# Two-part fp32r queries and keys, two heads at a time, for the first layer's cross attention

## The reference

```
x = x + mha(layernorm(x), ctx, ctx)      # first layer, 16 heads of 16 columns, 2048 keys
x = x + state_space(layernorm(x))        # a scan over the 128 rows
x = x + lora_mixture(layernorm(x))
x = x + single_head_attention(layernorm(x), ctx, mask)
x = x + windowed_attention(layernorm(x)) # 16 heads of 128
x = x + mixture_of_experts(layernorm(x)) # 8 experts
```

```
scores = qh @ kh.T / 4                   # 128 queries x 2048 keys, 16 columns deep
scores = where(ki <= qi + 1920, scores, -10000)
out    = softmax(scores) @ vh
```

## Time and profile before

| | us |
|---|---|
| median of 3 runs | 516.42 (515.78 to 519.46) |
| profiled execution, its own time | 518.79 |
| its span, first to last instruction | 516.8 |
| until pass one of group 0 starts | 30.8 |
| pass one of group 0 | 30.8 to 42.5 |
| groups 0 to 7 (pass two) | 42.5 to about 203 |
| PE busy, share of the span | 427.5, 83% |
| DVE busy | 344.4, 67% |
| ACT busy | 269.2, 52% |
| POOL busy | 121.6, 24% |

### The profile page before, as it was taken

How to read it: one execution, slowest core, us unless ns; L and a number is a source line. 1 busy time by engine, 2 the same in 40 slices (tenths; PEclk the granted TensorE clock), 3 DMA queues, 4 the chain that set the end, 5 groups by cost and what they waited for, 6 DMA issues and landing times.

```text
span 516.8 us, 8974 instructions
## 1 busy us (share of the span) xinstructions
PE 427.5 (83%) x3584; PEld 312.8 (61%) x3584; DVE 344.4 (67%) x544; ACT 269.2 (52%) x577; POOL 121.6 (24%) x78
## 2 busy tenths in 40 slices
PE   0177899998787796595989998999599889999997
PEld 0124466665554574434843373445588789999996
DVE  4952766777477964599754756585553599778772
ACT  4314678774678433360313242456784066777762
POOL 4010157000057000090001326241300112333300
PEclk9999889998798699667999999999799979999999
DMA  6599454433510053100740000004900097540000
GB/s 215 132 287 313 153 144 109 114 94 83 129 31 1 1 193 146 51 0 0 305 186 1 1 0 3 0 0 142 346 3 2 18 351 255 192 164 1 2 2 20
DMA packets 27306, 54.11 MB, mean 105 GB/s; under 512 B 5018, under 2 KB 17530, under 8 KB 23931
## 3 DMA queue, kind: packets, MB, share of 16 engines
q1 hardware_dynamic: 27264, 53.54, 32.7%
HBM read 40.65 MB, written 0.26 MB: 79 GB/s over the span
## 4 chain that ended last, share of the span: by engine, by line
PE 57%; DVE 26%; ACT 7%; issue 6%; DMA 2%; POOL 1%; SPq 0%; ACTq 0%; DVEq 0%; POOLq 0%
PE ps L1246 17%; PE ps L1067 8%; DVE mx L1632 5%; PE ps L882 5%; PE ps L869 4%; PE ps L838 3%; DVE reg_b L1423 3%; DVE reg_a L1423 2%; PE ps L1211 2%; ACT reg_b L653 2%; PE ps L1200 2%; PE ps L1201 2%; PE ps L977 1%; PE ps L996 1%; DVE reg_b L1414 1%
## 5 line engine op out<-in xcount | busy, mean ns | idle before, releaser
L1632 DVE TENSOR_REDUCE mx<-ps 128x1 f32<-128x1024 f32 x64 | 76.6, 1221 | 47.7 <-PE ps L838 37.1
L653 ACT ACTIVATE reg_b<-ps 128x512 f32<-128x512 f32 x128 | 75.3, 598 | 41.8 <-PE ps L869 21.9
L869 PE MATMUL ps<-qreg,reg_b 98*128 98x128 bf16 x512 | 51.2, 237 | 5.8 <-ACT reg_b L653 4.5
L869 PEld LDWEIGHTS ps<-qreg,reg_b 98*128 98x128 bf16 x512 | 38.2, 106 | 17.7 <-ACT reg_b L653 7.8
L1246 PE MATMUL ps<-part_a 128*128 128x256 f32 x384 | 48.2, 283 | 0.4 <-DVE part_a L1777 0.4
L1067 PE MATMUL ps<-reg_b,xT 128*128 128x512 f32 x96 | 47.6, 618 | 0.0
L1246 PEld LDWEIGHTS ps<-part_a 128*128 128x128 f32 x384 | 46.9, 192 | 0.6 <-DVE part_a L1777 0.6
L882 PE MATMUL ps<-reg_b 128*32 128x128 f32 x1024 | 46.3, 302 | 0.0
L838 PE MATMUL ps<-reg_b,qreg 96*128 96x512 bf16 x96 | 35.9, 443 | 9.0 <-DVE mx L1632 6.6
L788 ACT ACTIVATE reg_a<-ps,b 128x256 f32<-128x256 f32 x64 | 30.2, 471 | 23.9 <-PE ps L1246 23.9
L377 POOL TENSOR_TENSOR rstd<-ve,cf 128x1 f32<-128x1 f32 x12 | 6.7, 561 | 147.4 <-DVE ve L1319 147.3
(11 more groups left out here) (278 smaller groups left out, 891.6 us busy)
## 6 DMA issues: line engine op xcount, KB each, us to landing
reg_b<-in_w SPq DMA_DIRECT2D x16, 512.0 KB, 7.2
reg_b<-in_w SPq DMA_DIRECT2D x8, 1024.0 KB, 7.1
reg_b<-reg_b SPq DMA_DIRECT2D x56, 128.0 KB, 2.8
reg_b<-in_w_qkv SPq DMA_DIRECT2D x3, 2048.0 KB, 13.2
reg_b<-reg_a SPq DMA_DIRECT2D x40, 128.0 KB, 2.5
reg_a<-in_ctxK SPq DMA_DIRECT2D x4, 1024.0 KB, 7.2
reg_a<-in_ctx SPq DMA_DIRECT2D x2, 2048.0 KB, 10.0
reg_a<-in_ctxT SPq DMA_DIRECT2D x2, 2048.0 KB, 9.7
```

The source lines that it names most:

```text
L653: sc.activation(pT[n % 3], score_b[n % 2], ACT.Exp).then_inc(S("exp_done"), 1)
L869: mm = pe.matmul(cols, kS[g % 3][0:SROWS, c // 8, j, P * (c % 8):P * (c % 8 + 1)], qT[b][0:SROWS, HPG * hg + j, :], start=not last, stop=True)
L1632: ve.reduce_max(mx[:, piece // 2, piece % 2:piece % 2 + 1], score_a[m % 2].rearrange("p i k -> p (i k)"), X_AXIS).then_inc(S("max_done"), 1)
```

## The change

- Q and K are split in two float32r parts, high and low, instead of three bf16 parts. (float32r is a float32 that PE takes in a faster and less exact way.) One head takes 64 rows (`SLOT`): 16 rows whose first two hold ones in K and the negative maximum in Q (the other 14 are zero in Q), then K high by Q high, K high by Q low, K low by Q high. Two heads fill 128 rows.
- `scores_for_max(g, piece)` has 8 pieces, each two heads by 512 keys: one product on rows 0 to 63 and one on rows 64 to 127, into different banks. In the last quarter the mask is 256 columns wide and the products are two of 256 columns for each head. The pieces are issued in four portions of two: `MAX_AT` is `[(-1, 2), (1, 2), (3, 2), (5, 2)]`.
- `scores_shifted` has 2 products of 256 columns for a chunk in place of 4 of 128.
- K's parts: one ACT copy and one DVE subtraction for each half. For batch 1 one ACT copy and one POOL subtraction, four pieces each. SP issues 6 DMAs of 256 KB a group, with group 0's cut in two sets of 6 of 128 KB, so that pass one can start on the first two heads. The three small loads of ones go; in their place DVE sets one `kS` buffer to 1 and POOL the other two, and POOL sets two more tiles of 2048 words to 0.
- Only batch 0's queries are split and transposed (8 transposes of 128x128 float32) ahead of the first group. Batch 1's are split behind group 0's maximum and transposed and copied in groups 2, 3 and 4.

```
-MAX_AT = [(-1, 2), (0, 2), (1, 3), (2, 2), (3, 2), (4, 3), (5, 2)]
-FIRST_AT = [(3, 4), (4, 4), (5, 4), (6, 4)]
+MAX_AT = [(-1, 2), (1, 2), (3, 2), (5, 2)]
+FIRST_AT = [(3, 2), (4, 2), (5, 2), (6, 2)]
...
+            def spread_keys(g, pairs, pieces, name):
+                b, hg = divmod(g, NHG)
+                sp.wait_ge(S("k_high_done"), pieces)
+                for t in range(1, TERMS):
+                    if t == TERMS - 1:
+                        sp.wait_ge(S("k_low_done"), pieces)
+                    src = k_high_raw if t < TERMS - 1 else k_low_raw
+                    for j in range(2):
+                        row = SLOT * j + HD0 * t
+                        sp.dma_start(kS_raw[g % 3][row:row + HD0, pairs, :],
+                                     src[2 * hg + j::2 * NHG, b, pairs, :]).then_inc(S(name), 16)
...
             for g in range(NG):
-                b, hg = divmod(g, NHG)
                 if g >= 3:
                     sp.wait_ge(S("pv_done"), NCH * (g - 2))
-                for part, at in enumerate(((0, 3, 5), (1, 4), (2,))):
-                    sp.wait_ge(S(f"k{part + 1}_done"), (2, 2 + HPG)[b])
-                    for t in at:
-                        for half in range(2):
-                            row = 2 * hg + half
-                            sp.dma_start(kS[g % 3][t:QROWS:PARTS, half, :, :],
-                                         ks3[b][part][row::2 * NHG, :, :]).then_inc(S(f"kS_in{g % 3}"), 16)
+                if g == 0:
+                    sp.wait_ge(S("first_pads"), 1)
+                    spread_keys(0, slice(0, 1), 1, "first_in")
+                    spread_keys(0, slice(1, 2), 2, "kS_in0")
+                else:
+                    if g < 3:
+                        sp.wait_ge(S("pads_set"), 2 + g)
+                    spread_keys(g, slice(0, PAIRS), PAIRS if g < NHG else PAIRS + HPG, f"kS_in{g % 3}")
...
-            for i in range(2):
-                pool.memset(va[i][:, :, :, :], 0.0).then_inc(S("cleared"), 1)
+            pool.memset(part_o[:, :].bitcast(F32), 0.0).then_inc(S("pads_set"), 1)
+            pool.memset(part_q[:, :].bitcast(F32), 0.0).then_inc(S("pads_set"), 1)
+            pool.memset(kS_raw[1], 1.0).then_inc(S("pads_set"), 1)
...
             inv_sqrt(0, 0)
             inv_sqrt(0, 1)
+            pool.memset(kS_raw[2], 1.0).then_inc(S("pads_set"), 1)
+            for i in range(2):
+                pool.memset(va[i][:, :, :, :], 0.0).then_inc(S("cleared"), 1)
...
+            def key_high(u):
+                sc.wait_ge(S(f"ctxK_in{u}"), 16)
+                sc.copy(k_high[:, 0, u, :], ctxK[:, 0, u, :]).then_inc(S("k_high_done"), 1)
...
+            def query_rows(n):
+                sc.wait_ge(S("pads_set"), 2)
+                sc.wait_ge(S("qT_ps"), n + 1)
+                first, count, src = query_slots(n)
+                for j in range(2):
+                    rows = slice(SLOT * j, SLOT * (j + 1))
+                    sc.copy(qT[rows, first:first + count, P * j:P * (j + 1)],
+                            src[rows, :].rearrange("p (s q) -> p s q", s=count)).then_inc(S("qT_sb"), 1)
...
+            def scores_for_max(g, piece):
+                hg = g % NHG
+                u, quarter = divmod(piece, 4)
+                m = 8 * g + piece
...
+                if m >= 2:
                     pe.wait_ge(S("max_done"), m - 1)
+                dst = score_a[m % 2]
+                if quarter == 3:
+                    for j in range(2):
+                        pe.matmul(dst[:, j, 256:512], identb, hide_q, start=True, stop=False)
+                for at in (slice(256, 512), slice(0, 256)) if quarter == 3 else (slice(0, 512),):
+                    keys = slice(512 * quarter + at.start, 512 * quarter + at.stop)
+                    for j in range(2):
+                        rows = slice(SLOT * j, SLOT * (j + 1))
+                        mm = pe.matmul(dst[:, j, at], qT[rows, PAIRS * hg + u, P * j:P * (j + 1)], kS[g % 3][rows, u, keys],
+                                       start=quarter < 3 or at.start == 0, stop=True)
+                mm.then_inc(S("score_a"), 1)
...
-                for j in range(HPG):
-                    cols = score_b[n % 2][:, P * j:P * (j + 1)]
+                for u in range(PAIRS):
+                    cols = score_b[n % 2][:, 2 * P * u:2 * P * (u + 1)]
                     if last:
-                        pe.matmul(cols, identb, hide_k, start=True, stop=False)
-                    mm = pe.matmul(cols, kS[g % 3][0:SROWS, c // 8, j, P * (c % 8):P * (c % 8 + 1)], qT[b][0:SROWS, HPG * hg + j, :],
-                                   start=not last, stop=True)
+                        pe.matmul(cols.rearrange("p (j q) -> p j q", j=2), identb, hide_k, start=True, stop=False)
+                    mm = pe.matmul(cols, kS[g % 3][:, u, P * c:P * (c + 1)],
+                                   qT[:, PAIRS * (g % NHG) + u, :], start=not last, stop=True)
...
-            beside = {(0, 9): [(late_part1, 0)], (0, 11): [(late_part1, 1)], (0, 13): [(late_part1, 2)], (0, 15): [(late_part1, 3)],
-                      (1, 7): [(late_part2, 0)], (1, 9): [(late_part2, 1)], (1, 11): [(late_part2, 2)], (1, 13): [(late_part2, 3)],
+            beside = {(0, 13): [(late_high, 0)], (0, 15): [(late_high, 1)], (1, 1): [(late_high, 2)], (1, 3): [(late_high, 3)],
+                      (2, 8): [(query_rows, 2)], (2, 13): [(query_rows, 3)], (3, 8): [(query_rows, 4)], (4, 7): [(query_rows, 5)],
...
+            ve.memset(kS_raw[0], 1.0).then_inc(S("first_pads"), 1)
             ve.wait_ge(S("x_in"), 32)
             layer_norm(0)
...
+                ve.wait_ge(S("pads_set"), 1)
                 q = tmp[b][:, :].rearrange("p (h d) -> p h d", h=H0)
                 link(ve.tensor_scalar(tmp[b][:, :], xn[b][:, :], 1.0 / math.sqrt(HD0), None, ALU.mult))
+                link(ve.tensor_copy(q_split[b][:, :, 1:4:2, :], q.unsqueeze(2).to_broadcast([P, H0, 2, HD0])))
+                ve.tensor_tensor(q_split[b][:, :, 2, :], q, q_split[b][:, :, 1, :], ALU.subtract)\
                     .then_inc(S("q_split"), 1)
...
-            key_residue(0)
+            key_low(0)
             split_queries(0)
-            key_residue(1)
-            key_part3(0)
-            key_part3(1)
-            split_queries(1)
+            key_low(1)
...
-                    ve.reduce_max(mx[:, piece // 2, piece % 2:piece % 2 + 1],
-                                  score_a[m % 2].rearrange("p i k -> p (i k)"), X_AXIS).then_inc(S("max_done"), 1)
+                    u, quarter = divmod(piece, 4)
+                    ve.reduce_max(mx[:, 2 * u:2 * u + 2, quarter:quarter + 1], score_a[m % 2], X_AXIS)\
+                        .then_inc(S("max_done"), 1)
```

More of the change, by code:

```diff
@@ L29 @@
 NG = NB * NHG
[L30 to L34 removed]
+PAIRS = 2
+SLOT = P // PAIRS
+TERMS = SLOT // HD0
+KEY_DMAS = 2 * (TERMS - 1)
 VW = 32
@@ L404, in state_input @@
                 pool.wait_ge(S("bc_sb"), (8, 20)[b])
+                if b == 0:
+                    for i in range(3):
+                        pool.wait_ge(S(f"kS_in{i}"), 16 * KEY_DMAS * (3, 3, 2)[i])
                 pool.tensor_tensor(state[b][:, h], tmp[b][:, h * P:(h + 1) * P].unsqueeze(1).to_broadcast([P, NS, P]),
@@ new lines, in query_columns @@
+            def query_columns(n):
+                pe.wait_ge(S("q_split"), (1, 1, 2, 2, 2, 2)[n])
+                if n >= 2:
+                    pe.wait_ge(S("o_all"), (2, 2, 3, 4)[n - 2])
+                    pe.wait_ge(S("qT_sb"), 2 * n)
+                first, count, dst = query_slots(n)
+                q = q_raw[n // 2 if n < 2 else 1].rearrange("p (s j) t d -> p s (j t d)", j=2)
+                for i in range(count):
+                    mm = pe.transpose(dst[:, P * i:P * (i + 1)], q[:, first + i, :], ident)
+                mm.then_inc(S("qT_ps"), 1)
@@ L1022, in side_work @@
                     step[0](*step[1:])
-            for part in range(16):
-                scores_for_max(0, part)
+            for piece in range(8):
+                scores_for_max(0, piece)
             max_to_rows(0)
```

194 lines of the change are left out of this document (71 added, 123 removed).

## The result

The changed kernel takes **533.98 us** (median of 4 runs, 532.31 to 536.48) against 517.94 (515.78 to 521.34) for the kernel before: a ratio of 1.031 (95% interval 1.023 to 1.039). It is slower. The forecast was 499, with 0.03 for slower. Its profiled execution took 535.1 us, the span 533.3. Medians are over all runs of a kernel; a ratio compares only its undisturbed ones with those of the kernel before, so the two can differ by some tenths of a per cent.

The account below looks back on a forecast made before the run. It took the uncovered first 42.5 us and then mostly PE in the groups as bounds. Start -12.8 and groups -5.0 make -17.8: 518.8 profiled gives 501.0, forecast 499 us from the 516.4 median; range 487 to 510.

Parts of the forecast that it names:

- What covers the rest of the start: Loads behind the start: values and later keys at 310 GB/s arrive in time, with a cover of 1 to 6 us.
- part 1: Start of the kernel: first product at 17.1 us, transposes of the maxima at 29.8 instead of 42.55, -12.8 us.
- the sum: All groups together -5 us, with group 0 -0.5 and group 1 -1.5; with the start's -12.8, -17.8 in all.
- the DMA queue paces the start: Rival at the start: load covers missed by 9 us in all, giving 508 us; chance 0.05.
- slower rival: Pass one: 64-row float32r products go at plain float32's rate, giving about 596 us; chance 0.03.
- The clock rival: Group borders: PE's waits bring the half clock at four more borders, +12 us, giving 511; chance 0.13.
- The memsets ... on POOL end by about 17 and cost nothing: Start: POOL's memsets of the last `kS` buffer and of `va` end by about 17 us, at no cost.
- Part 2: Pass one on PE: row halves overlap 1.65-fold, -1.2 us a group, against +0.8 for changes into and out of halves.
- halves one after the other: Rival in pass one: the row halves do not overlap, +1.4 us a group, giving 506; chance 0.12.
- Part 3: Pass two's scores: 2 x 256 columns a chunk instead of 4 x 128 cost 0, bounds -0.5 and +0.8 a group.
- Part 4: Four portions in pass one: two reductions follow the last instead of one, +0.7 us a border, for six borders.

Follow-up runs that it names:

- run 5: Changed kernel with each head's terms interleaved over 48 rows and POOL's memsets moved behind the keys' subtractions (also written e5): 511.49 us, ratio 0.987.
- run 1: Changed kernel with only each head's three terms interleaved over 48 rows instead of 16 adjacent rows each (also written e1): 515.94 us, ratio 1.000.
- bf16 stand-in: Run 5 with pass two's score products reading a bf16 unit matrix on both sides, so its scores are not computed: 504.44 us, ratio 0.973.
- reverse edit: Run 5 with pass one's pieces issued in seven visits instead of four portions of two: 504.70 us, ratio 0.974.
- the edit in the old kernel: Kernel before with only its table changed, 16 parts of pass one in four visits of four instead of seven: 521.56 us, ratio 1.006.
- Version 6: Changed kernel with terms spread over 48 rows, POOL's memsets later and seven visits instead of four: 504.70 us, ratio 0.974.

## Why the prediction was wrong

**The step that failed is "What covers the rest of the start"**, with the landing in part 1. It took the landing of a K copy, 2.8 us, from `reg_b<-reg_b SPq DMA_DIRECT2D x56, 128.0 KB`, a row of copies to every sixth row, and carried the 310 GB/s of the earlier trace rows over to copies to 16 adjacent rows. What the runs showed in its place: 174 and 181 GB/s, batch 1's values landed after 35.9 us, and group 2's keys there at 68.2, forecast for 42.6 (61.2 with the memsets late, so most of the delay isn't theirs). I read the size and the number of the transfers in the diff (6 of 256 KB for 12 of 128) and not their rows. The keys came late for groups 1 and 2, PE waited 3.4 and 5.3 us, and the clock did the rest: groups 0 and 1 took 16.0 us more than before, where the sum had -2.0. Undone by itself this gives back 18 us by the medians, 16 by the ratios. Even with the spread rows and the start as forecast (run 5) group 2's keys land at 48.3, 6 us after the forecast: 310 GB/s was too high for them too, but nothing waited. The rival "the DMA queue paces the start" named the right mechanism, at 0.05 and for 9 us, as a gain missed; it could turn the sign, and that case was absent. My slower rival was about float32r in pass one. The clock rival didn't happen at the borders: with the rows spread (run 1), a wait of 1.4 us at the border of groups 0 and 1 left the clock at 1.00, and in the kernel after it is low behind the waits for keys.

**"The memsets ... on POOL end by about 17 and cost nothing"**: they do end at 16.2, and DVE is held until 16.37: 5.6 us at the maximum of group 0 with the slow rows (35.3 to 29.7) and 6.5 without (35.6 to 29.1). I had allowed for a factor of 1.7 on DVE's steps from the two scans; two operations of 0.41 us that last 7.58 are no slowdown by a factor but a wait for the other's end. The Trainium skill ("SBUF — State Buffer", Who interferes with whom) calls the shared port pair an exclusive lock, held for a whole instruction, that a `tensor_scalar` can take. The trace agrees that DVE is shut out rather than slowed, and shows it shut out through three memsets in a row. With the memsets moved, first product and maximum came at 16.1 and 29.2, against 17.1 and 29.8 forecast: the rest of part 1 came out within 1 us, partly by luck: I read 11.43 us for 12 issues as 0.95 each, but an issue takes 0.6, and 4 us of the 11.43 are SP's wait for a part of the keys in the middle of the twelve. The measured start, -7.2, lies outside the bounds that I had given it (-8.5 to -15).

**Part 2** was right in its first half: 0.165 us a product of 512 columns where full-width ones take 0.23, so 1.4-fold for two halves (1.65 forecast); "halves one after the other" is refuted. The price of leaving the halves fits as well: 0.32 us from the last pair's start to the next visit, where 512 columns alone take 0.23, so about 0.1.

**Part 3**, priced at 0, costs 0.13 us a pair (0.67 against 0.54), 1.0 a group at the full clock, just outside its bound of +0.8. The bf16 stand-in returned 7.0 us by the medians, part of it perhaps by way of the clock, and 0.6 to 0.7 in each group at the full clock.

**Part 4** was priced at +0.7 a border, about 4 in all. The reverse edit gave 4.4 in the groups (0.5 to 0.8 in each one at the full clock) and 6.8 in the medians, the edit in the old kernel cost 3.1: right in size. Its place was partly another: ACT's idle 1.15 us behind a masked portion.

**The sum, mended.** The medians make a ladder: 533.98 after, 515.94 with the rows spread (-18.0), 511.49 with the memsets late (-4.5), 504.44 with the bf16 stand-in (-7.0). The first two steps weren't measured side by side; the ratios to the kernel before (1.031, 1.000, 0.987, 0.973) make the steps about 16, 7 and 8 us. The last stands 5.4 above the forecast; 1.5 of that is that the kernel before has 517.9 in these runs and 516.4 in the three I started from. For the other 4 its borders say where, not why: the start gained 13.7 (12.8 forecast), the groups 1.8 (5 forecast), and behind the groups, where the code is the same, it is 2.2 us longer. Version 6, which keeps the float32r products, has the start as forecast (-13.3 by its borders) and 0 in sum over the groups, where I had -5.

**What stays open.** Whether the fullest port is the cause of the transfers' three classes: the order fits, the sizes only roughly, and no run varies the source rows. Why e5's group 6 is 1 us longer than e1's.

## What to carry to other kernels

Read the rows of an SBUF copy like its bytes: a landing time from the profile holds for the layout it was measured with, and a slow copy delays the loads behind it on the queue most of all. Where POOL gets large memsets at the start, look at which DVE steps run beside them, and move them behind the chain that PE waits for. When a change frees time on one engine, ask whether what feeds it next can come earlier too; here late operands cost 8.7 us of waiting, and groups 0 and 1 lost 16.9 against the run with the rows spread; the rest came with the low clock behind the waits.

## What the runs showed of the hardware

- Destination rows of a 256 KB SBUF-to-SBUF copy: 16 adjacent rows 2.6 us a copy in a back-to-back set, every 3rd 2.3, every 2nd, 4th, 6th, 7th or 8th 1.6 to 1.75. In the kernel a full queue moves 174 GB/s with adjacent rows and 285 with every 3rd.
- A `tensor_scalar` of 0.41 us took 7.06 beside three memsets of POOL (3.5, 1.8 and 1.8 us), and 0.41 again with them moved.
- Four 64-row float32r products of 512 columns, two on each row half: 0.66 us until the next visit, 0.165 each; the two of a pair start together.
- A 128x128 weight load: 212 ns in float32r, 99 in bf16, means over eight groups; 190 and 97 at the full clock.
- A memset of 4096 words takes 3.47 us on DVE and 3.51 on POOL.
